# Attention scores over the 32 rows of a head pair, head-tile scores issued in turn with the next pair's tail-tile scores

## The chip, the cores and the metric

The kernel runs on one core of a Trainium2 chip. The metric is the time of one execution on the device, in microseconds (us), and the median of several runs is compared. The engines are called TensorE (PE in the profile, with its weight loads as PEld), VectorE (DVE), ScalarE (ACT), GpSimd (POOL) and SyncE (SP).

## What is computed

One block of a transformer in the "macaron" form: half a mixture-of-experts feed-forward, attention, and half the same feed-forward again. The input is 4 batches x 256 tokens x 256 features. The change touches the attention alone:

```
q = (x @ w_q.T).reshape(b, t, 16, 16)      # 16 heads of 16 features
k = (x @ w_k.T).reshape(b, t, 16, 16)
v = (x @ w_v.T).reshape(b, t, 16, 16)
scores = einsum('bqhd,bkhd->bhqk', q, k)
scores = where(causal, -inf, scores)
attn = softmax(scores / sqrt(256), axis=-1)
ctx = einsum('bhqk,bkhd->bqhd', attn, v).reshape(b, t, 256)
x = x + ctx @ w_o.T + b_o
```

## The kernel before

**Stages.** The first feed-forward fills the span up to about 175 us, the attention lies between 175 and 303 us, and the second feed-forward follows. Each engine has its own instruction list, written out by hand; a list is worked off in its order, and `wait_ge` on a semaphore holds an engine's list until another engine has counted far enough. `reach(eng, signal, count)` is the same wait, left out where the count is zero or less.

**Attention.** A batch has 256 queries and keys, which are two tiles of 128 queries. The first is called the head tile here: it sees 128 keys at most. The second, the tail tile, sees all 256. The 256 features of q and k lie on partitions in two chunks `c` of 128; a chunk holds 8 heads of 16 rows, so four pairs of heads (`CPAIRS` = 4), and a batch has 8 pairs (`HPAIRS`). Products in full precision are made from three matmuls: high part times high part, high times low, low times high.

**Steps.** `sweep` runs `step` for batch 0 on its own, in a loop for batches 1 to 3 (with the rest of the batch before in it), and once more for what is left. A step handles pieces of several pairs, shifted against each other. In step `s` TensorE does, in this order:

- `scores(b, s, True)`: the tail scores of pair `s - 2` (`SLAG` is 2), three matmuls of 512 columns at line 1483 (two heads x 256 keys) into bank 0 or 1, and the causal mask as a fourth matmul at line 1484;
- `turn_probs`: six transposes (line 1494) of the probabilities of pair `s - 4`;
- in steps 0 and 3, `chunk`: eight matmuls (line 1450) for a chunk of q and k of the next batch into bank 7;
- `scores(b, s, False)`: the head scores of pair `s - 2`, three matmuls of 256 columns and a mask into bank 2;
- `weigh`: 18 small matmuls (lines 1509 to 1511) of probabilities and values of pair `s - 5`.

In step 6 follow four transposes of the context (`turn_context`, line 1523) and at the start of step 7 eight matmuls of the output projection (`project_out`, line 1530).

**The other engines in a step.** VectorE: maximum of the tail scores (line 1143), maximum of the head scores (1147), and `low` (1156), the low parts of the turned probabilities; in step 5 first `add_up` (1164, 1166). ScalarE, in this order: `exps` of the tail (line 787, two instructions and their accumulator reads), in steps 0 and 3 the copies of k and q (773, 774), `exps` of the head (line 795, likewise two), then `high` (line 805), which copies the turned probabilities of the pair that TensorE turns in step `s + 1`. In step 6 the context's copy (line 815) comes ahead of the tail's exponentials. GpSimd: `mask_keys` (line 617) makes `k_head` for a pair, four instructions for high and low part and the two heads. The stationary operand is a whole chunk of q, 128 rows, so `k_head` holds the chunk's keys with all rows but the head's 16 set to zero (`head_mask`). Two slots of `k_head` are used in turn (`KSLOTS`).

**Buffers.** The tail scores have banks 0 and 1 in turn, the head scores bank 2 alone. The waits that follow from it in `scores` are

```
reach(pe, tail_probs_ready, g * 2 - 2)     # tail: the pair before the last has left its bank
reach(pe, head_probs_ready, g * 2)         # head: the last pair's exponentials have read bank 2
```

where `g` counts the pairs and each pair counts the semaphore up by two, once for each head.

Of the kernel before, what the change touches and what calls it, by code (L numbers as in the profile page):

```python
# [54 lines left out]
CONSTS = 20  # L55
IDENT_CONSTS = 3
KSLOTS = 2
# [7 lines left out]
SUM_STEP, OUT_STEP = 5, 6  # L65
POOL_LEAD = 1
# [9 lines left out]
def build(nc, x_in, wq_in, wk_in, wv_in, wo_in, bo_in, wr_in, win_in, wout_in, bias_in, out):  # L76
    with ExitStack() as ctx:
# [21 lines left out]
        with ExitStack() as room:  # L99
# [8 lines left out]
            with ExitStack() as inner_room:  # L108
                k_head = [inner_room.enter_context(nc.sbuf_tensor(f"k_head{u}", [P, 2, 2, SEQ], F32R)) for u in range(KSLOTS)]
# [90 lines left out]
        head_mask = sb("head_mask", [P, HPC])  # L200
        minus_half = sb("minus_half", [P, TILES])
# [258 lines left out]
        def _(pool):  # L460
# [44 lines left out]
            select(head_mask[:, :], [[HD, HPC]], HD - 1, -1, ALU.is_ge, 0.0)  # L505
            assert steps[0] == CONSTS

# [97 lines left out]
            def mask_keys(b, s):  # L605

                g = b * HPAIRS + (s - SLAG)
                p = (s - SLAG) % HPAIRS
                c = p // CPAIRS
                chunks = (b * DK + (c + 1 - (DK if s < SLAG else 0)))  # L610

                reach(pool, head_scored, g + (1 - KSLOTS))
                for part, (k, ready) in enumerate(((k_hi, k_hi_ready), (k_lo, k_lo_ready))):
                    pool.wait_ge(ready, chunks)
                    for hh in range(2):
                        h = 2 * p + hh
# [20 lines left out]
        def _(act):  # L637
# [139 lines left out]
            def exps(b, s, tail):  # L777

                g = b * HPAIRS + (s - SLAG)
                p, u = (s - SLAG) % HPAIRS, s % 2  # L780
                batch = b if s >= SLAG else b - 1
# [27 lines left out]
            def step(b, old, new):  # L809
                for s in range(HPAIRS):  # L810
# [14 lines left out]
                    if old if s < SLAG else new:  # L825
                        exps(b, s, False)
# [26 lines left out]
        def _(dve):  # L853
# [282 lines left out]
            def maxima(b, s, tail):  # L1136

                g = b * HPAIRS + (s - SLAG)
                u = s % 2
# [50 lines left out]
            def step(b, old, new):  # L1190
                for s in range(HPAIRS):
# [6 lines left out]
                    if old if s < SLAG else new:  # L1198
# [46 lines left out]
        def _(pe):  # L1245
# [217 lines left out]
            def scores(b, s, tail):  # L1463

                g = b * HPAIRS + (s - SLAG)
                c, u = (s - SLAG) % HPAIRS // CPAIRS, s % 2
                keys = k_head[s % KSLOTS]
# [153 lines left out]
```

## Time and profile before

| | us |
|---|---|
| median of three runs | 452.99 |
| the three runs | 454.75, 452.99, 451.97 |
| span of the profiled execution | 448.6 |
| TensorE busy | 401.3 (89%) |
| VectorE busy | 302.4 (67%) |
| GpSimd busy | 269.0 (60%) |
| ScalarE busy | 257.7 (57%) |

The span goes from the first to the last instruction; the profiled execution's own device time isn't given apart, so the span is set beside the median, which is 4.4 us above it. Matmuls overlap, and their ends are modelled: the distance between the starts of two matmuls says more than the busy time.

### The profile page before, as it was taken

Reading aid. Unit: us, or ns where it says so; the run is one execution under the profiler, and the core shown is the slowest. Engines: PE = TensorE matmul, PEld = TensorE weight load, DVE = VectorE, ACT = ScalarE, POOL = GpSimd, SP = SyncE. Lnnn points to the kernel's source line nnn. Section 1 sums busy time; section 2 is a strip of 40 time slices with the busy share of each in tenths; the row PEclk is TensorE's granted clock in tenths of the full one; section 3 lists DMA queues with packets and bytes.
Section 4 is the critical chain, followed back from the end, with each engine's and each line's share of the span. In section 5 each row is a group of like instructions: output and inputs, shape, how many; then the busy total and the mean of one; then the engine's idle time right before and its main releaser. Section 6 shows DMA issues by size and latency. Waiting matters only on the chain.

```text
span 448.6 us, 10288 instructions
## 1 busy us (share of the span) xinstructions
PE 401.3 (89%) x2892; PEld 330.1 (74%) x2893; DVE 302.4 (67%) x605; ACT 257.7 (57%) x630; POOL 269.0 (60%) x314
## 2 busy tenths in 40 slices
PE   7305999999999989889999999988899999999995
PEld 3302788888888876758788888766478888888884
DVE  6795855685565688697767677775556576655656
ACT  2561656555655645688778788832065565565552
POOL 5846874686547817857757777410255576755760
PEclk9555899999999999999999999998899999999999
DMA  8748841111212180000000000004571112211136
GB/s 276 287 187 300 282 136 58 47 57 37 70 49 49 43 273 8 1 1 3 4 0 0 0 0 0 1 1 153 162 249 53 54 35 70 59 58 47 47 85 222
DMA packets 25736, 38.87 MB, mean 87 GB/s; under 512 B 3056, under 2 KB 20720, under 8 KB 25712
## 3 DMA queue, kind: packets, MB, share of 16 engines
q1 hardware_dynamic: 19088, 24.41, 16.1%
q0 software_dynamic: 4544, 12.07, 8.9%
q10 hardware_dynamic: 2080, 2.10, 1.4%
q8 instruction: 12, 0.20, 0.2%
q14 instruction: 12, 0.10, 0.1%
HBM read 29.37 MB, written 9.19 MB: 86 GB/s over the span
## 4 chain that ended last, share of the span: by engine, by line
PE 65%; DVE 16%; DMA 7%; POOL 3%; ACT 3%; issue 3%; SPq 0%; DVEq 0%; ACTq 0%; POOLq 0%
PE bank L1326 24%; PE bank L1348 12%; PE bank L1483 7%; PE bank L1494 4%; PE bank L1336 4%; DMA arena<-xn_scratch,gather_row 3%; PE bank L1450 2%; PE bank L1302 2%; PE bank L1249 2%; DMA w_out<-y_scratch 2%; PE bank L1530 2%; DVE w_lo L892 2%; POOL w_lo L511 2%; DMA y_scratch<-arena,scatter_row 1%; PE bank L1484 1%
## 5 line engine op out<-in xcount | busy, mean ns | idle before, releaser
L524 POOL DMA_INDIRECT arena<-xn_scratch,gather_row x46 | 52.8, 1149 | 58.1 <-PE bank L1302 35.6
L530 POOL DMA_INDIRECT y_scratch<-arena,scatter_row x42 | 59.3, 1412 | 31.6 <-ACT arena L701 28.6
L1326 PE MATMUL bank<-w_hi,xT_hi 128*128 x184 | 62.4, 420 | 2.1 <-ACT xT_hi L664 2.1
L1018 DVE TENSOR_TENSOR wo_lo<-w_out,wo_hi 128x1024 fp32r<-128x1024 f32 x46 | 62.0, 1348 | 2.9 <-PE bank L1348 2.0
L1023 DVE TENSOR_TENSOR gT_lo<-bank,gT_hi 128x512 fp32r<-128x512 f32 x46 | 31.7, 690 | 45.4 <-ACT gT_hi L679 45.4
L1326 PE MATMUL bank<-w_lo,xT_hi 128*128 x184 | 58.0, 396 | 0.0
L1326 PE MATMUL bank<-w_hi,xT_lo 128*128 x184 | 57.8, 395 | 0.0
L617 POOL TENSOR_TENSOR k_head<-k_hi,head_mask 128x256 fp32r<-128x256 f32 x64 | 38.8, 627 | 28.8 <-PE bank L1484 21.7
L690 ACT ACTIVATE wo_hi<-w_out 128x1024 fp32r x46 | 48.8, 1061 | 9.5 <-issue 8.7
L672 ACT ACTIVATE arena<-bank 128x512 f32<-128x512 f32 x46 | 27.5, 598 | 42.9 <-PE bank L1326 42.9
L1007 DVE TENSOR_TENSOR xT_lo<-bank,xT_hi 128x256 fp32r<-128x256 f32 x46 | 19.5, 424 | 43.0 <-ACT xT_hi L664 43.0
L1483 PE MATMUL bank<-k_head,xT_hi 128*128 128x256 f32 (+1 forms) x128 | 39.8, 392 | 1.9 <-ACT probs L795 1.2
L1326 PEld LDWEIGHTS bank<-w_hi,xT_lo 128*128 128x128 f32 x184 | 34.8, 189 | 8.3 <-DVE xT_lo L1007 0.2
L1326 PEld LDWEIGHTS bank<-w_lo,xT_hi 128*128 128x128 f32 x184 | 34.8, 189 | 8.0
L617 POOL TENSOR_TENSOR k_head<-k_lo,head_mask 128x256 fp32r<-128x256 f32 x64 | 38.3, 620 | 0.6 <-DVE k_lo L1130 0.6
L701 ACT ACTIVATE arena<-bank 128x256 f32<-128x256 f32 x42 | 16.2, 385 | 39.1 <-PE bank L1348 39.1
L787 ACT ACTIVATE probs<-bank,neg_max 128x256 f32<-128x256 f32 x64 | 29.9, 479 | 8.7 <-DVE neg_max L1143 8.6
L1348 PE MATMUL bank<-wo_hi,gT_hi 128*128 128x256 f32 x184 | 33.0, 301 | 1.4 <-ACT gT_hi L679 1.4
L805 ACT ACTIVATE pT_hi<-bank 128x384 f16<-128x384 f32 x64 | 28.0, 488 | 10.4 <-PE bank L1494 10.3
L1156 DVE SCALAR_TENSOR_TENSOR pT_lo<-bank,pT_hi 128x384 f16<-128x384 f32 x64 | 32.4, 548 | 0.6
L1326 PEld LDWEIGHTS bank<-w_hi,xT_hi 128*128 128x128 f32 x184 | 29.0, 194 | 3.5 <-issue 3.1
L1032 DVE TENSOR_TENSOR arena<-arena,bank 128x512 f32<-128x512 f32 x46 | 31.1, 677 | 0.4 <-issue 0.4
(180 smaller groups left out, 979.9 us busy)
## 6 DMA issues: line engine op xcount, KB each, us to landing
w_out<-in_win_t SPq DMA_DIRECT2D x8, 1024.0 KB, 5.1
w_out<-in_wout_t SPq DMA_DIRECT2D x16, 512.0 KB, 6.0
w_out<-y_scratch SPq DMA_DIRECT2D x16, 256.0 KB, 4.4
xn_scratch<-arena ACTq DMA_DIRECT2D x2, 1024.0 KB, 6.1
x<-in_x SPq DMA_DIRECT2D x4, 256.0 KB, 3.7
out<-x SPq DMA_DIRECT2D x4, 256.0 KB, 2.2
arena<-xn_scratch,gather_row POOLq DMA_INDIRECT x46, 3.4
y_scratch<-arena,scatter_row POOLq DMA_INDIRECT x46, 3.0
```

What stands on the lines that cost most here:

```text
L524: pool.indirect_dma_start(out=xb[j % 2][:, :], out_offset=None, in_=xn_dram, in_offset=bass.IndirectOffsetOnAxis(ap=gather_row[:, j:j + 1] ...
L530: pool.indirect_dma_start(out=y_dram, in_=y[j % 2][:, :], in_offset=None, out_offset=bass.IndirectOffsetOnAxis(ap=scatter_row[:, j:j + 1], ...
L617: ins = pool.tensor_tensor(k_head[s % KSLOTS][:, part, hh, :], k[:, c, :].bitcast(F32), head_mask[:, h % HPC:h % HPC + 1].to_broadcast([P, ...
L690: act.activation(wo_hi[u][:, :, :], w_out[:, bass.ds(e, 1), :, :].rearrange("p o c d -> p (o c) d"), ACT.Copy)\
L787: act.activation(probs[u][:, hh, 1:3, :], bank[u][:, hh * SEQ:(hh + 1) * SEQ].rearrange("p (k t) -> p k t", k=2), ACT.Exp, bias=neg_max[u] ...
L1018: dve.tensor_tensor(wo_lo[:, :, :], w_out[:, bass.ds(e, 1), :, :].rearrange("p o c d -> p (o c) d"), wo_hi[u][:, :, :].bitcast(F32), ALU.s ...
L1023: dve.tensor_tensor(gT_lo[:, :, :], bank[4][:, :].rearrange("p (c t) -> p c t", c=HK), gT_hi[:, :, :].bitcast(F32), ALU.subtract).then_inc ...
L1032: dve.tensor_tensor(g[:, :], sa[:, :], bank[2 + u][:, :], ALU.mult).then_inc(g_done, 1)
L1156: dve.scalar_tensor_tensor(pT_lo[u][:, :, :], bank[3 + hh][:, 0:3 * P].rearrange("p (k t) -> p k t", k=3), P_SCALE, pT_hi[u][:, :, :], ALU ...
L1326: last = pe.matmul(bank[2 * half + u][:, :], tok[u][:, k, :], wts[:, bass.ds(e, 1), k, half * H:(half + 1) * H], start=(part == 0 and k == ...
L1348: last = pe.matmul(bank[y_bank(j)][:, 0:D], tok[:, c, :], wts[:, c, :], start=(part == 0 and c == 0), stop=(part == 2 and c == HK - 1))
L1483: pe.matmul(to, q[:, 1 if tail else 0, :], keys[:, part, :, 0:width], start=(n == 0), stop=False)
```

## The change

Four edits:

- `k_head` is now made for a chunk, not for a pair. `parity_mask` has two columns: ones in the rows of all even heads, and ones in those of all odd heads. `mask_keys(b, c)` runs in steps 0 and 3 only, four instructions for four pairs. Three small GpSimd instructions at the start build the mask (`CONSTS` goes from 20 to 23). `k_head` has one buffer for each chunk, as large in all as before.
- The scores are products over the 32 rows of the pair within the chunk: both operands are cut to `rows`. Other pairs' rows are left out by the cut, the other head of the pair by the mask.
- The head scores come one step later (`HEAD_LAG` = 1): step `s` has the tail scores of pair `s - 2` and the head scores of pair `s - 3`, whose maxima and exponentials move by one step with them.
- Both are issued by one call at the start of the step: first all waits of both, then tail, head, tail, head, tail, head, tail mask, head mask. The pairs of a step are neighbours, so they lie in different groups of 32 rows.

```diff
-            def mask_keys(b, s):
-                g = b * HPAIRS + (s - SLAG)
-                p = (s - SLAG) % HPAIRS
-                ...
-                reach(pool, head_scored, g + (1 - KSLOTS))
+            def mask_keys(b, c):
+                reach(pool, head_scored, b * HPAIRS + (CPAIRS * (c + 1) - HPAIRS))
                 for part, (k, ready) in enumerate(((k_hi, k_hi_ready), (k_lo, k_lo_ready))):
-                    pool.wait_ge(ready, chunks)
+                    pool.wait_ge(ready, b * DK + (c + 1))
                     for hh in range(2):
-                        ins = pool.tensor_tensor(k_head[s % KSLOTS][:, part, hh, :], k[:, c, :].bitcast(F32),
-                                                 head_mask[:, h % HPC:h % HPC + 1].to_broadcast([P, SEQ]), ALU.mult)
+                        ins = pool.tensor_tensor(k_head[c][:, part, hh, :], k[:, c, :].bitcast(F32),
+                                                 parity_mask[:, hh:hh + 1].to_broadcast([P, SEQ]), ALU.mult)
...
-                    if old if s < SLAG else new:
-                        mask_keys(b, s)
+                    if new and s in CHUNK_STEP:
+                        mask_keys(b, CHUNK_STEP.index(s))
...   # ScalarE's exps and VectorE's maxima
-                g = b * HPAIRS + (s - SLAG)
+                at = s - SLAG - (0 if tail else HEAD_LAG)
+                g = b * HPAIRS + at
...
-                    if old if s < SLAG else new:
+                    if old if s < SLAG + HEAD_LAG else new:
                         exps(b, s, False)
...
+            def scores(b, s, tail, head):
                 mask = bc(neg_mask[:, :], 1, [P, 2, P])
+                jobs = []
                 if tail:
+                    at = s - SLAG
+                    g, p = b * HPAIRS + at, at % HPAIRS
+                    chunks = b * DK + (p // CPAIRS + 1 - (DK if at < 0 else 0))
+                    if p % CPAIRS == 0:
+                        pe.wait_ge(qk_ready, chunks)
+                        pe.wait_ge(k_head_ready, chunks)
                     reach(pe, tail_probs_ready, g * 2 - 2)
+                    jobs.append((bank[s % 2][:, :].rearrange("p (h k) -> p h k", h=2), p, 1, SEQ, tail_scored))
+                if head:
+                    at = s - SLAG - HEAD_LAG
+                    g, p = b * HPAIRS + at, at % HPAIRS
                     reach(pe, head_probs_ready, g * 2)
+                    jobs.append((bank[2][:, 0:2 * P].rearrange("p (h k) -> p h k", h=2), p, 0, P, head_scored))
+                for n, (q, part) in enumerate(((q_hi, 0), (q_hi, 1), (q_lo, 0))):
+                    for to, p, tile, width, _ in jobs:
+                        c, rows = p // CPAIRS, slice(p % CPAIRS * ROWS, p % CPAIRS * ROWS + ROWS)
+                        pe.matmul(to, q[c][rows, tile, :], k_head[c][rows, part, :, 0:width], start=(n == 0), stop=False)
+                for to, _, _, width, scored in jobs:
+                    pe.matmul(to[:, :, width - P:width], ident_b[:, :], mask, start=False, stop=True).then_inc(scored, 1)
...   # TensorE's step
-                    if old if s < SLAG else new:
-                        scores(b, s, True)
+                    scores(b, s, old if s < SLAG else new, old if s < SLAG + HEAD_LAG else new)
...   # after chunk(...)
-                    if old if s < SLAG else new:
-                        scores(b, s, False)
```

## Rows read from the trace of the kernel before

**Rows 1.** Page, part 1: busy time of each engine.
```profile
PE 401.3 (89%) x2892; PEld 330.1 (74%) x2893; DVE 302.4 (67%) x605; ACT 257.7 (57%) x630; POOL 269.0 (60%) x314
```
**Rows 2.** Windows: length, busy time and (instructions) of each engine, PEclk, DMA share, GB/s.
```profile
202.00:216.00 14.00, 14.00 (x147) 11.78 (x145) 9.96 (x20) 12.22 (x49) 9.70 (x17) 1.00 0.01 2
...
300.00:380.00 80.00, 75.99 (x462) 60.85 (x463) 47.48 (x116) 36.89 (x65) 37.44 (x30) 0.96 0.34 109
```
**Rows 3.** Timeline of TensorE, steps 1 and 2 of batch 1: start us, us, what.
```profile
206.96 0.71 PE L1483 MATMUL bank<-k_head,xT_hi 128*128 128x512 f32 x2
...
207.74 0.28 PE L1484 MATMUL bank<-neg_mask,ident_b 128*128 128x256 bf16 x1
207.86 0.82 PE L1494 MATMUL bank<-ident,probs 128*128 128x128 f32 x6
208.44 0.48 PE L1483 MATMUL bank<-k_head,xT_hi 128*128 128x256 f32 x2
...
208.88 0.28 PE L1484 MATMUL bank<-neg_mask,ident_b 128*128 128x256 bf16 x1
...
209.45 0.71 PE L1483 MATMUL bank<-k_head,xT_hi 128*128 128x512 f32 x2
...
211.00 0.50 PE L1483 MATMUL bank<-k_head,xT_hi 128*128 128x256 f32 x2
```
**Rows 4.** Timeline of ScalarE, same steps.
```profile
208.47 0.87 ACT L805 ACTIVATE pT_hi<-bank 128x384 f16<-128x384 f32 x2 [0.41 <-PE bank L1494]
...
209.23 0.48 ACT L787 ACTIVATE probs<-bank,neg_max 128x256 f32<-128x256 f32 x1
...
210.13 0.38 ACT L795 ACTIVATE probs<-bank,neg_max 128x128 f32<-128x128 f32 x1
...
210.72 0.23 ACT L795 ACTIVATION_READ_ACCUMULATOR probs<-bank,neg_max  x1
```
**Rows 5.** Timeline of VectorE, same steps.
```profile
208.17 0.69 DVE L1143 TENSOR_REDUCE neg_max<-bank 128x2 f32<-128x512 f32 x1 [0.38 <-PE bank L1484]
```
**Rows 6.** Waits of TensorE, 176 to 292 us: total us, times, longest.
```profile
PE bank L1483 <- ACT probs L795: 1.2, 1, 1.2
```
**Rows 7.** Timeline of TensorE, step 5 of batch 1: first small matmul, next tail scores.
```profile
221.50 0.19 PE L1509 MATMUL bank<-v,pT_hi 128*128 x1
...
222.82 0.49 PE L1483 MATMUL bank<-k_head,xT_hi 128*128 128x512 f32 x1
```
**Rows 8.** Timeline of TensorE and ScalarE, step 3 of batch 1: the chunk.
```profile
213.92 1.03 PE L1450 MATMUL bank<-arena,wq 128*128 x4
...
215.85 0.39 ACT L773 ACTIVATE k_hi<-bank 128x256 fp32r<-128x256 f32 x1 [0.20 <-PE bank L1450]
...
216.13 0.38 ACT L774 ACTIVATE xT_hi<-bank 128x256 fp32r<-128x256 f32 x1
```
**Rows 9.** Timeline of ScalarE, step 6 of batch 1: the context's copy.
```profile
225.10 0.60 ACT L815 ACTIVATE wv<-bank 128x512 f32<-128x512 f32 x1
225.58 0.49 ACT L787 ACTIVATE probs<-bank,neg_max 128x256 f32<-128x256 f32 x1
```
**Rows 10.** Timeline of TensorE: first tail scores of step 0, batch 1 and last sweep.
```profile
202.69 0.71 PE L1483 MATMUL bank<-k_head,xT_hi 128*128 128x512 f32 x2
...
284.87 0.71 PE L1483 MATMUL bank<-k_head,xT_hi 128*128 128x512 f32 x2
```
**Rows 11.** Timeline of TensorE and ScalarE, batch 0: tail scores of step 6, step 5's last exponentials.
```profile
195.77 0.71 PE L1483 MATMUL bank<-k_head,xT_hi 128*128 128x512 f32 x2
...
198.86 0.21 ACT L795 ACTIVATION_READ_ACCUMULATOR probs<-bank,neg_max 128x1 f32 x1
```
**Rows 12.** Timeline of TensorE, last sweep: last pair's probabilities turned.
```profile
292.92 0.99 PE L1494 MATMUL bank<-ident,probs 128*128 128x128 f32 x6
```
**Rows 13.** Page, part 5: a group of the key masks, count, busy us, mean ns, idle before.
```profile
L617 POOL TENSOR_TENSOR k_head<-k_hi,head_mask 128x256 fp32r<-128x256 f32 x64 | 38.8, 627 | 28.8 <-PE bank L1484 21.7
```
**Rows 14.** Timeline of GpSimd at the start: constants done, first work after them.
```profile
12.40 0.45 POOL L472 TENSOR_SCALAR_AFFINE_SELECT head_mask<-head_mask 128x8 f32<-128x8 f32 x2
13.52 7.94 POOL L511 TENSOR_TENSOR w_lo<-w_out,w_hi 128x1024 fp32r<-128x1024 f32 x3 [0.66 <-ACT w_hi L657]
```

More of the change, by code:

```diff
@@ L54 @@
 STAGES = 3
-CONSTS = 20
+CONSTS = 23
 IDENT_CONSTS = 3
-KSLOTS = 2
+ROWS = 2 * HD
 P_SCALE = 2.0 ** 15
@@ L65 @@
 SUM_STEP, OUT_STEP = 5, 6
+HEAD_LAG = 1
 POOL_LEAD = 1
@@ L108, in build @@
             with ExitStack() as inner_room:
-                k_head = [inner_room.enter_context(nc.sbuf_tensor(f"k_head{u}", [P, 2, 2, SEQ], F32R)) for u in range(KSLOTS)]
+                k_head = [inner_room.enter_context(nc.sbuf_tensor(f"k_head{c}", [P, 2, 2, SEQ], F32R)) for c in range(DK)]
             xnT_late = room_sb("xnT_late", [P, DK, T])
@@ L505, in _ @@
             select(head_mask[:, :], [[HD, HPC]], HD - 1, -1, ALU.is_ge, 0.0)
+            then(pool.tensor_tensor(parity_mask[:, :], head_mask[:, 0:2], head_mask[:, 2:4], ALU.add))
+            for h in range(4, HPC, 2):
+                then(pool.tensor_tensor(parity_mask[:, :], parity_mask[:, :], head_mask[:, h:h + 2], ALU.add))
             assert steps[0] == CONSTS
@@ L777, in exps @@
             def exps(b, s, tail):
-                g = b * HPAIRS + (s - SLAG)
-                p, u = (s - SLAG) % HPAIRS, s % 2
-                batch = b if s >= SLAG else b - 1
+                at = s - SLAG - (0 if tail else HEAD_LAG)
+                g = b * HPAIRS + at
+                p, u = at % HPAIRS, at % 2
+                batch = b if at >= 0 else b - 1
                 if tail:
@@ L1136, in maxima @@
             def maxima(b, s, tail):
-                g = b * HPAIRS + (s - SLAG)
-                u = s % 2
+                at = s - SLAG - (0 if tail else HEAD_LAG)
+                g = b * HPAIRS + at
+                u = at % 2
                 if tail:
@@ L1197, in step @@
                         low(b, s)
-                    if old if s < SLAG else new:
+                    if old if s < SLAG + HEAD_LAG else new:
                         maxima(b, s, False)
@@ L1461, in values @@
                     last.then_inc(v_done, 1)
[L1463 to L1467, printed above, removed]
+            def scores(b, s, tail, head):
                 mask = bc(neg_mask[:, :], 1, [P, 2, P])
+                jobs = []
                 if tail:
-                    if (s - SLAG) % CPAIRS == 0:
-                        pe.wait_ge(qk_ready, b * DK + (c + 1 - (DK if s < SLAG else 0)))
-                    pe.wait_ge(k_head_ready, g + 1)
+                    at = s - SLAG
[4 more added lines that the diff above has]
+                        pe.wait_ge(k_head_ready, chunks)
@@ L1475, in scores @@
                     reach(pe, tail_probs_ready, g * 2 - 2)
-                    to = bank[u][:, :].rearrange("p (h k) -> p h k", h=2)
-                else:
+                    jobs.append((bank[s % 2][:, :].rearrange("p (h k) -> p h k", h=2), p, 1, SEQ, tail_scored))
+                if head:
+                    at = s - SLAG - HEAD_LAG
+                    g, p = b * HPAIRS + at, at % HPAIRS
                     reach(pe, head_probs_ready, g * 2)
-                    to = bank[2][:, 0:2 * P].rearrange("p (h k) -> p h k", h=2)
@@ L1481, in scores @@
-                width = SEQ if tail else P
-                for n, (q, part) in enumerate(((q_hi[c], 0), (q_hi[c], 1), (q_lo[c], 0))):
-                    pe.matmul(to, q[:, 1 if tail else 0, :], keys[:, part, :, 0:width], start=(n == 0), stop=False)
-                pe.matmul(to[:, :, width - P:width], ident_b[:, :], mask, start=False, stop=True)\
-                    .then_inc(tail_scored if tail else head_scored, 1)
+                    jobs.append((bank[2][:, 0:2 * P].rearrange("p (h k) -> p h k", h=2), p, 0, P, head_scored))
```

5 lines of the change are left out of this document (1 added, 4 removed).

## The prediction

> **What bounds the kernel now.** I read the page first: TensorE is busy for 89% of the span, far ahead of the others [rows 1]. That is a mean, so I cut the span into windows by stage. In the attention's loop TensorE shows 14.00 us of work in 14.00 us at the full clock, ScalarE 12.22 and VectorE 9.96 [rows 2]. Read alone, this says: take work from TensorE. The timeline of one step tells how far that holds. Tail scores start at 206.96 and the next step's at 209.45, which is 2.49 us; inside, tail matmuls take 0.78, their mask 0.12, the transposes 0.58, the head's three matmuls 0.44, all as distances between starts [rows 3]. So TensorE issues without a gap and paces this step.
>
> The same rows show a second thing, and the forecast rests on it. The tail scores that start at 206.96 are followed by VectorE's maximum, which begins at 208.17 [rows 5]; ScalarE first does the copies of the turned probabilities (208.47), then the exponentials of these tail scores (209.23), then those of the head scores (210.13), and the last accumulator read ends at 210.72 + 0.23 = 210.95 [rows 4]. The head scores of the *next* step start at 211.00 [rows 3]: they wait for bank 2 to be read. From tail scores of one step to head scores of the next the chain takes 4.04 us. It fits in a 2.49 us rhythm because the head scores stand 1.48 us into their step (208.44 - 206.96), behind transposes that have something else to do: 2.49 + 1.48 = 3.97 are on offer, and 4.04 are wanted. It is just met; in one place of batch 0 it isn't, and TensorE waits 1.2 us for those exponentials [rows 6].
>
> **The change part by part.**
>
> *The moved wait.* The new `scores` first waits for everything that tail and head need, and then issues both. One of these waits is `head_probs_ready` for the pair before: ScalarE's head exponentials of step s-1. ScalarE makes them behind the tail exponentials of step s-1, and these need the tail scores of step s-1. Hence the scores of step s can't start before the whole chain from the scores of step s-1 has run. Queued behind that wait on TensorE are the next tail scores, the transposes, the chunk and the small matmuls; ScalarE's copies wait for the transposes, and its next tail exponentials stand behind the copies. The lag of one step doesn't help: it moves maxima and exponentials along with the head scores. What was 4.04 us spread over one step and the 1.48 us of the next becomes a cycle that closes once a step.
>
> *Its length in a plain step*, counted from the start of the scores:
> - Scores to transposes. If the head matmuls run inside the tail's, it is 0.78 + 0.12 + 0.12 = 1.02 [rows 3]. If they run one after the other, 0.44 more: 1.46. No row shows matmuls over 32 rows, nor a change from such a form to the 128-row masks. A bound for one change is what a matmul still has in the array when the next starts: the mask lasts 0.28 and is followed after 0.12, so 0.16; into the 32-row form TensorE comes from a wait, out of it at full cost. Bounds: 0.90 (head mask hidden too) to 1.46 + 2 x 0.16 = 1.78. I take 1.02 + 0.16 = 1.18, as the two jobs have different rows and banks.
> - First transpose to ScalarE's copy: 208.47 - 207.86 = 0.61; copies until tail exponentials: 209.23 - 208.47 = 0.76 [rows 3, 4]. The tail's maximum isn't later: scores' mask at 0.78, VectorE 0.43 behind its start, 0.69 long, gives 1.90 [rows 3, 5] against 1.18 + 1.37 = 2.55.
> - Tail and head exponentials: 210.95 - 209.23 = 1.72 [rows 4]; back to TensorE 211.00 - 210.95 = 0.05 [rows 3, 4].
>
> Sum: 1.18 + 0.61 + 0.76 + 1.72 + 0.05 = 4.32 us, against 2.49. TensorE's own work in it is 1.18 + 0.58 and the small matmuls. Those took 1.32 us for 18 where TensorE had no instructions queued (221.50 to 222.82 [rows 7]), so they end at about 3.1 us and are hidden.
>
> The Trainium skill bears on the first item twice. "TensorE: Matmul & The Clock Gate", Part 3: Packing small matmuls, has matmuls in different 32-row strips start some 4 ns apart; "TensorEngine Tiling (Array Packing)", Key Properties, says that changing the tiling mode drains the engine, which speaks against a kernel that goes in and out of it once a step. By the first alone the item is 1.02, and the second has no price there. No row of this trace shows either.
>
> *Chunk steps (0 and 3).* ScalarE's copies of k and q stand between tail and head exponentials and wait for the chunk's matmuls: these start after the transposes, at 1.18 + 0.58 = 1.76; the first copy is 215.85 - 213.92 = 1.93 behind, two copies take twice 216.13 - 215.85 = 0.28 [rows 8]; then 0.82 for the head exponentials (210.95 - 210.13 [rows 4]) and 0.05. Sum 5.12.
>
> *Step 6.* The context's copy stands ahead of the tail exponentials and delays them by 225.58 - 225.10 = 0.48 [rows 9]: 4.80. The output projection falls into TensorE's free time.
>
> *One pass of the loop:* 5 x 4.32 + 2 x 5.12 + 4.80 = 36.64 us. Before: (284.87 - 202.69) / 3 = 27.39 [rows 10]. That is +9.25, and +27.7 for three passes. VectorE's `add_up` in step 5, which held the small matmuls of [rows 7] back, is now hidden; the absolute sum has this in it.
>
> *Batch 0.* Until step 5 VectorE's work on the values sets the pace in both kernels. The scores of step 6 then wait for step 5's head exponentials, which end at 198.86 + 0.21 = 199.07, some 0.6 earlier without head scores in step 2 (an estimate), where the tail scores started at 195.77 [rows 11]: +2.7. Steps 6 and 7 take 2 x 4.32 = 8.64 in place of 202.69 - 195.77 = 6.92: +1.7. Together +4.4.
>
> *Last sweep.* From step 0 to the turning of the last pair's probabilities it was 292.92 - 284.87 = 8.05 [rows 10, 12]. Now two steps (8.64), the head scores alone with mask and one change (0.44 + 0.12 + 0.16), transposes to copies to exponentials (0.61 + 0.76 + 0.82) and 0.05: 11.60, so +3.5. All of the rest up to the second feed-forward hangs on it.
>
> *Key masks.* GpSimd made 128 instructions of some 0.62 us [rows 13] and now makes 32. That frees about 60 us, none of it on the path: GpSimd idled ahead of them, waiting for head scores. A chunk's four take 2.5 us and are needed two steps later in step 2, three steps later in step 6. Zero, and a slight gain on VectorE at most.
>
> *Three constants at the start.* GpSimd idles 0.66 us between the last constant and the first weight split [rows 14]; the last two constants took 0.45 together, so three take some 0.68. Zero, and at most these 0.68 if the split doesn't wait for ScalarE as it does now.
>
> **Sum.** 27.7 + 4.4 + 3.5 = 35.6. The profiled span becomes 448.6 + 35.6 = 484.2, and by the median, 4.4 above the span, 452.99 + 35.6 = 488.6 us.
>
> **Rivals.**
>
> *A. TensorE stays the bound, and the head matmuls vanish inside the tail's.* This is the reading of [rows 1, 2], and where the skill's overlap would lead if nothing else closed: 0.44 x 32 steps = 14 us, 439 us. It decides if the exponentials of step s-1 are over before TensorE reaches the scores of step s, so if the chain were at most 2.05 us (2.49 - 0.44). The rows give 4.04 for the chain as it is. Against it: everything. For it: only that I could misread an order. Chance 0.04. Changed within 1% (chain loosely met, gains and losses cancel): 0.03.
>
> *B. The matmuls over 32 rows run one after the other, with drains both ways.* The step is 4.32 + (1.78 - 1.18) = 4.92. Over 24 steps of the loop, and about 5 around it, 0.60 x 29 = 17 us more: 506 us. For it: no row of this trace shows two matmuls side by side in the array. Chance 0.20. In this case most of the scores' rows in the trace would start one tail or head length apart.
>
> *C. The clock falls.* TensorE would be idle for a third of each step. In 300 to 380 us, where routing leaves it idle, the mean granted clock is 0.96 in place of 1.00 [rows 2]. At the lower level (1.2 GHz) scores and transposes of a step, 1.18 + 0.3 before ScalarE's first copy, would take twice as long: +1.5 x 29 = 43 us, 532 us. Against it: idle stretches of 1.2 us a step are short, and work comes back each time. Chance 0.05.
>
> *D. The chain as forecast*, with the scores' item anywhere between 0.90 and 1.4: chance 0.68. Its own range: 0.90 makes 0.28 x 29 = 8 us less, 480; a shorter chain where GpSimd is quiet takes 3 more, 477; the upper end 0.22 x 29 = 6 more, 495.
>
> **How the numbers follow.** Slower by over 1%: D, B and C, 0.93. A measurement of this kernel can tell about 1% from no change. The range leaves out A, the null and C, some 0.12, and reaches over B: 477 to 506.
>
> **What the profile of the changed kernel would show.** Tail scores 4.3 us apart in plain steps and 5.1 in steps 0 and 3; once a step TensorE idle ahead of its scores, released by ScalarE's head exponentials (`probs`); a chain that changes engine four times a step (TensorE scores and transposes, ScalarE) in place of TensorE alone; GpSimd's masks at 32. Tail and head matmuls starting close together show the overlap (else B). The feed-forwards must be unchanged. The prediction is wrong if steps run under 4 us, or if the head exponentials end before TensorE has finished its small matmuls.

## The result and the profile after

| | before | after |
|---|---|---|
| median, us | 452.85 (4 runs, 451.97 to 454.75) | 524.12 (4 runs, 522.11 to 525.93) |
| profiled span, us | 448.6 | 523.3 |
| mean granted clock of TensorE | 0.954 | 0.840 |

The ratio is 1.159, with a 95% interval of 1.155 to 1.163. The change costs 71 us; 35.6 were forecast, and the time lies above the range of 477 to 506. The direction and the new cycle came as forecast; the other half of the loss is TensorE's clock, which the sum had left at full speed.

**The page.** TensorE's busy time [rows 1], the clock in 40 slices, the shares of the chain, one group of key masks [rows 13] and the scores' group:

```profile
PE 434.4 (83%) x2892; PEld 352.9 (67%) x2893; DVE 304.2 (58%) x605; ACT 260.0 (50%) x630; POOL 213.5 (41%) x221
...
PEclk9556999999999995766766675775879999999999
...
PE 61%; DVE 13%; ACT 10%; DMA 7%; issue 5%; POOL 3%; ACTq 1%; SPq 0%; DVEq 0%; POOLq 0%
...
L1488 PE MATMUL bank<-k_head,xT_hi 32*128 32x256 f32 (+1 forms) x128 | 32.5, 509 | 47.1 <-ACT probs L795 46.9
...
L616 POOL TENSOR_TENSOR k_head<-k_hi,parity_mask 128x256 fp32r<-128x256 f32 x16 | 9.5, 615 | 123.2 <-ACT k_hi L772 123.2
```

TensorE has the same 2892 instructions as before and is busy for 33 us more: that points to the same work at a lower speed. The clock row shows where. In the slices from 196 us to the end of the last scores it reads 5 to 7 in place of 9. The last two rows show that the scores' matmuls wait 47 us in all for ScalarE's head exponentials, and that a group of masks is down from 64 instructions to 16.

**Windows by stage**, columns as in [rows 2]. First the loop of the kernel before, from step 0 of batch 1 on; then the changed kernel's batch 0, loop and last sweep:

```profile
202.70:284.80 82.10, 81.41 (x856) 67.70 (x852) 57.98 (x120) 66.02 (x256) 59.34 (x103) 1.00 0.00 1
```
```profile
180.30:211.10 30.80, 22.40 (x154) 17.05 (x154) 18.41 (x36) 18.59 (x69) 4.82 (x5) 0.74 0.01 1
211.20:352.10 140.90, 105.44 (x852) 83.38 (x852) 60.71 (x120) 67.53 (x255) 17.54 (x30) 0.68 0.00 0
352.20:367.40 15.20, 11.53 (x95) 8.96 (x95) 7.19 (x16) 6.92 (x26) 0.00 (x0) 0.50 0.01 1
```

Of the 74.7 us between the spans, 58.9 lie in the loop, 6.7 in batch 0 (24.1 to 30.8), 7.2 in the last sweep (8.0 to 15.2), 1.7 before the attention and 0.2 behind it. VectorE's and ScalarE's busy time in the loop is nearly that of before (60.7 for 58.0, 67.5 for 66.0); TensorE's rises from 81.4 to 105.4 at a mean clock of 0.68.

**The timeline of TensorE** shows two steps in a row, as [rows 3]; of the small matmuls only the last one of the first step is shown:

```profile
235.74 0.70 PE L1488 MATMUL bank<-k_head,xT_hi 32*128 32x512 f32 x4 [1.10 <-ACT probs L795]
236.08 0.59 PE L1488 MATMUL bank<-k_head,xT_lo 32*128 32x256 f32 x2
236.60 0.39 PE L1490 MATMUL bank<-neg_mask,ident_b 128*128 128x256 bf16 x2
236.83 0.82 PE L1499 MATMUL bank<-ident,probs 128*128 128x128 f32 x6
...
237.92 0.18 PE L1516 MATMUL bank<-v,pT_lo 128*128 x1
240.06 1.19 PE L1488 MATMUL bank<-k_head,xT_hi 32*128 32x512 f32 x4 [1.97 <-ACT probs L795]
...
241.61 0.61 PE L1490 MATMUL bank<-neg_mask,ident_b 128*128 128x256 bf16 x2
242.01 1.49 PE L1499 MATMUL bank<-ident,probs 128*128 128x128 f32 x6
...
245.78 0.76 PE L1488 MATMUL bank<-k_head,xT_hi 32*128 32x512 f32 x2 [1.80 <-ACT probs L795]
```

The first step takes 240.06 - 235.74 = 4.32 us, to the hundredth what was forecast. Scores to transposes are 1.09 in it (1.18 forecast): 0.86 for six products, 0.23 for two masks. Its last small matmul ends at 237.92 + 0.18 = 238.10, and TensorE then waits for 1.97 us. The second step takes 5.72 with the same instructions. Its products last 1.55, its masks 0.40, its transposes 1.49 in place of 0.82. The first step up to 239.60 and the second as windows:

```profile
235.74:239.60 3.86, 2.35 (x32) 1.86 (x32) 2.58 (x6) 2.16 (x9) 1.28 (x3) 1.00 0.01 2
240.06:245.78 5.72, 3.92 (x32) 3.06 (x33) 2.52 (x6) 2.59 (x10) 1.20 (x2) 0.50 0.01 3
```

The granted clock is 1.00 in the first and 0.50 in the second, the lower of the two levels (1.2 GHz). Each step has one block of tail and head scores; 19 of the 32 ran wholly at the lower level.

**The chain of waits** through the slow step, in order of time (start, us, what):

```profile
240.06 1.62 PE bank L1488 x4
241.68 0.54 PE bank L1490 x2
242.22 1.29 PE bank L1499 x6
...
244.28 0.66 ACT probs L787 x3
244.94 0.71 ACT probs L795 x4
245.65 0.14 issue
245.78 0.58 PE bank L1488
```

It is the cycle of the prediction: scores, transposes, ScalarE's copies, tail exponentials, head exponentials, scores. Between transposes and exponentials ScalarE's queue works through the copies, in short pieces that are left out here. In this cycle 3.45 us lie on TensorE (1.62 + 0.54 + 1.29), so the work that the lower clock stretches lies on the path.

### The profile page after: what moved, and what is told of

Its sections match the earlier page's. It is cut to its first block, busy times and chain, and to the rows that moved or that the text cites. A ratio compares the mean times of both kernels' runs of the same rounds, so it can differ in the third digit from the quotient of the medians.

```text
span 523.3 us, 10163 instructions
## 1 busy us (share of the span) xinstructions
PE 434.4 (83%) x2892; PEld 352.9 (67%) x2893; DVE 304.2 (58%) x605; ACT 260.0 (50%) x630; POOL 213.5 (41%) x221
## 4 chain that ended last, share of the span: by engine, by line
PE 61%; DVE 13%; ACT 10%; DMA 7%; issue 5%; POOL 3%; ACTq 1%; SPq 0%; DVEq 0%; POOLq 0%
PE bank L1327 21%; PE bank L1349 11%; PE bank L1488 8%; PE bank L1499 6%; ACT probs L795 4%; ACT probs L787 4%; PE bank L1451 3%; PE bank L1337 3%; DMA arena<-xn_scratch,gather_row 3%; PE bank L1490 3%; PE bank L1303 2%; DMA w_out<-y_scratch 2%; PE bank L1535 2%; DVE arena L879 1%; POOL w_lo L516 1%
## 5 line engine op out<-in xcount | busy, mean ns | idle before, releaser
L1488 PE MATMUL bank<-k_head,xT_hi 32*128 32x256 f32 (+1 forms) x128 | 32.5, 509 | 47.1 <-ACT probs L795 46.9
L805 ACT ACTIVATE pT_hi<-bank 128x384 f16<-128x384 f32 x64 | 30.7, 490 | 81.5 <-PE bank L1499 79.3
L1144 DVE TENSOR_REDUCE neg_max<-bank 128x2 f32<-128x512 f32 x32 | 22.1, 691 | 72.1 <-PE bank L1490 72.1
L616 POOL TENSOR_TENSOR k_head<-k_hi,parity_mask 128x256 fp32r<-128x256 f32 x16 | 9.5, 615 | 123.2 <-ACT k_hi L772 123.2
L1488 PEld LDWEIGHTS bank<-k_head,xT_hi 32*128 32x128 f32 x128 | 14.5, 257 | 51.6 <-ACT probs L787 32.5
L1499 PE MATMUL bank<-ident,probs 128*128 128x128 f32 x192 | 42.0, 382 | 0.0
L1157 DVE SCALAR_TENSOR_TENSOR pT_lo<-bank,pT_hi 128x384 f16<-128x384 f32 x64 | 34.9, 556 | 10.7 <-ACT pT_hi L805 10.1
L1499 PEld LDWEIGHTS bank<-ident,probs 128*128 128x128 f32 x192 | 35.9, 205 | 1.4
```

The costliest lines, as they stand in the source:

```text
L805: act.activation(pT_hi[(s - 1) % 2 * 2 + hh][:, :, :], bank[3 + hh][:, 0:3 * P].rearrange("p (k t) -> p k t", k=3), ACT.Copy, scale=P_SCAL ...
L1157: dve.scalar_tensor_tensor(pT_lo[u][:, :, :], bank[3 + hh][:, 0:3 * P].rearrange("p (k t) -> p k t", k=3), P_SCALE, pT_hi[u][:, :, :], ALU ...
L1488: pe.matmul(to, q[c][rows, tile, :], k_head[c][rows, part, :, 0:width], start=(n == 0), stop=False)
L1499: last = pe.transpose(bank[3 + hh][:, i * P:(i + 1) * P], probs[s % 2][:, hh, i, :], ident[:, :])
```

## The experiments

Each kernel was run beside the kernel before on the same chip, and each ratio is against it; the rounds were on different chips, where the kernel before took 452.9 to 453.9 us. "128 rows" means that the products run over all rows of the chunk, so that scores of four pairs are summed; such a kernel is a probe and nothing to use.

### Is the cycle the chain through ScalarE, and what opens it?

**e4: head exponentials a step earlier.** ScalarE does them ahead of its copies, VectorE takes the head's maximum first; TensorE's list is that of the changed kernel.

```diff
@@ ScalarE's step @@
-                    if old if s < SLAG + HEAD_LAG else new:
-                        exps(b, s, False)
...
+                    if old if s + 1 < SLAG + HEAD_LAG else new:
+                        exps(b, s + 1, False)
                     if old if s < SLAG + 1 else new:
                         high(b, s)
@@ VectorE's step @@
+                    if old if s < SLAG + HEAD_LAG else new:
+                        maxima(b, s, False)
                     if old if s < SLAG else new:
                         maxima(b, s, True)
...
-                    if old if s < SLAG + HEAD_LAG else new:
-                        maxima(b, s, False)
```

> The changed kernel with another order on two engines: VectorE takes the head's maximum before the tail's, and ScalarE makes the head exponentials of a step ahead of the copies of turned probabilities and of the tail exponentials. The joint wait stays. Theory: the cycle now holds scores (head mask issued at 0.97), 0.43 to the head's maximum, 0.42 for it, 0.13 to ScalarE, 0.82 for the head exponentials and 0.05 back: 2.8 us in place of 4.32. Plain steps of 2.8 to 3.0 us, clock over 0.93, 446 to 460 us. Rival (it is not this order on ScalarE that stretches the step): steps stay over 4 us, 515 us or more.

Measured: 469.22 us, ratio 1.035 (1.030 to 1.040). ScalarE's timeline has the new order, and the scores of one step and the next are 2.79 apart:

```profile
211.77 0.36 ACT L795 ACTIVATE probs<-bank,neg_max 128x128 f32<-128x128 f32 x1
...
212.12 0.87 ACT L805 ACTIVATE pT_hi<-bank 128x384 f16<-128x384 f32 x2
212.86 0.49 ACT L787 ACTIVATE probs<-bank,neg_max 128x256 f32<-128x256 f32 x1
```
```profile
212.42 0.69 PE L1488 MATMUL bank<-k_head,xT_hi 32*128 32x512 f32 x4 [0.50 <-ACT probs L795]
...
215.21 0.69 PE L1488 MATMUL bank<-k_head,xT_hi 32*128 32x512 f32 x4
```

So moving the head's two exponentials on ScalarE, and its maximum on VectorE, takes 1.5 us out of a step: the cycle is what the theory says. The total missed the expected 446 to 460, as the loop's mean clock is 0.85 and steps 0, 3, 5 and 6 take longer than summed.

**e1: the old place, 32 rows.** The head scores go back behind the chunk and lose their lag.

```diff
-HEAD_LAG = 1
+HEAD_LAG = 0
...
-                    scores(b, s, old if s < SLAG else new, old if s < SLAG + HEAD_LAG else new)
+                    scores(b, s, old if s < SLAG else new, False)
...
                         chunk(b, CHUNK_STEP.index(s))
+                    scores(b, s, False, old if s < SLAG + HEAD_LAG else new)
```

> Theory (the joint wait closes a cycle over TensorE, VectorE and ScalarE once a step, and the idle time that it makes lets the clock fall): with the head scores back in their old place behind transposes and chunk, for the same pair as the tail scores and with a wait of their own, while products over 32 rows and masks by parity stay, the cycle is open again. Plain steps of 2.5 to 2.8 us, clock as in the kernel before (0.95 or more over the span), 450 to 462 us: two changes of form a step may cost up to 0.16 us each. Rival (products over 32 rows are themselves what slows TensorE or lowers its clock): clock under 0.90 and over 475 us.

Measured: 468.03 us, ratio 1.032 (1.026 to 1.038), between what the two expected. **e5** is the same with the lag of one step kept.

> The changed kernel with the head scores back in their old place and with a wait of their own, but still one step late. Theory: the lag alone closes a cycle too, a shorter one: the transposes of step s need the head exponentials of step s-1, so 0.61 from the transposes' start to ScalarE's copies, 0.76, 1.72 for the exponentials and 0.05 make plain steps of 3.14 to 3.25 us at the full clock, between the 2.97 of the run without the lag and the 4.32 of the changed kernel; 474 to 490 us with some of the steps at the lower clock. Rival (only the joint wait matters, the lag is free): steps as in the run without the lag (2.97) and 464 to 471 us.

Measured: 472.69 us, ratio 1.044 (1.039 to 1.048), between the two ranges. Its plain steps are 2.96 us, those of e1 2.95 to 2.97, and the expected 3.14 to 3.25 is wrong. It took the transposes of a step to wait for both of the last step's head exponentials. In the kernel the first three wait for the first head's and the last three for the second's. Tail scores of one step, its two head exponentials' last reads, and the transposes of the next:

```profile
257.33 0.49 PE L1488 MATMUL bank<-k_head,xT_hi 32*128 32x512 f32 x1
...
260.86 0.23 ACT L795 ACTIVATION_READ_ACCUMULATOR probs<-bank,neg_max  x1
...
261.20 0.23 ACT L795 ACTIVATION_READ_ACCUMULATOR probs<-bank,neg_max  x1
...
261.31 0.82 PE L1499 MATMUL bank<-ident,probs 128*128 128x128 f32 x6
```

The first head's end at 261.09, 0.22 ahead of the transposes at 261.31; the second head's end at 261.43, and the fourth transpose starts at 261.63. So the lag closes a chain that is some 0.2 us shorter than the step, and TensorE sets the step as in e1. It is the joint wait at the start of the step that closes the long cycle. The lag isn't free all the same: e5's loop takes 99.0 us at a mean clock of 0.91, e1's 95.6 at 0.94, and no run shows why the clock is lower with it.

e1's timeline shows where its 0.48 us over the old 2.49 lie, by the distances of [rows 3]:

```profile
256.74 0.72 PE L1488 MATMUL bank<-k_head,xT_hi 32*128 32x512 f32 x2
...
257.63 0.28 PE L1490 MATMUL bank<-neg_mask,ident_b 128*128 128x256 bf16 x1
257.75 0.82 PE L1499 MATMUL bank<-ident,probs 128*128 128x128 f32 x6
258.50 0.50 PE L1488 MATMUL bank<-k_head,xT_hi 32*128 32x256 f32 x2
...
259.04 0.28 PE L1490 MATMUL bank<-neg_mask,ident_b 128*128 128x256 bf16 x1
```

Tail products to mask 0.89 (was 0.78), transposes to head scores 0.75 (0.58), head products to mask 0.54 (0.44), and from the small matmuls into the tail scores 0.53 (0.45). At each change between 32 and 128 rows 0.08 to 0.17 us are lost; between products of the same form the distances are those of before, within 0.02 us.

**e7: e1 with all 128 rows** (`rows` is `slice(0, P)`), to see whether that is the cause.

> Head scores in their old place and no lag, masks by parity once a chunk, and products over all 128 rows (so the scores of a chunk's even or odd heads are added up and the output is not the reference's). The run with 32 rows in this order had plain steps of 2.97 where the kernel before has 2.49. Theory: the 0.48 us are four changes of form a step, 0.08 to 0.17 each; with 128 rows they are gone, plain steps of 2.49 to 2.55 us, 449 to 456 us, clock 0.95 or more. Rival (the 0.48 us come from the masks by parity or from GpSimd's new timing): steps stay at 2.8 to 3.0, 462 us or more.

Measured: 450.00 us over 10 runs, ratio 0.994 (0.991 to 0.997). Plain steps are 2.49 again, at a clock of 1.00 in the whole loop. The 18 us between e1 and e7 belong to the 32 rows alone, through the changes of form (0.48 us a step) and through the clock (0.94 in e1's loop). e7 is the changed kernel's key masks, three more constants and nothing else of the change: these cost nothing measurable, and the two together are 0.6% faster than the kernel before.

### Where do the other 37 us come from?

**e3: matmuls into the pause.** Seven matmuls that nobody reads go into bank 7 behind the small ones, in four of the eight steps.

```diff
                         weigh(b, s)
+                    if new and s in (1, 2, 4, 5):
+                        pe.wait_ge(qk_ready, b * DK + (1 if s < CHUNK_STEP[1] else 2))
+                        warm(7, 7)
```

> The changed kernel with seven matmuls of 512 columns on constants behind the small matmuls of steps 1, 2, 4 and 5 of batches 0 to 3, into bank 7, which is free there (about 1.5 us at the full clock, inside the idle time of some 2 us). Theory: TensorE's idle time is what lets the clock fall, so the granted clock returns to 0.93 or more over the span and the kernel comes to 486 to 500 us, near what was forecast for the cycle at the full clock. Rival (the clock falls for the form of the score matmuls, or the time is lost elsewhere): clock stays under 0.88, 520 us or more.

Measured: 505.99 us, ratio 1.115 (1.109 to 1.121), above the expected 486 to 500. The filled stretch holds (from step 2 to step 7 plain steps take 4.26 to 4.36), and the clock still falls at steps 0 and 1, ahead of which steps 6, 7 and 0 had nothing filled in.

**e8: the same in every step**, into the tail bank that is free, more or fewer by the step's pause.

```diff
+                    if (new and (old or s >= 2)) or (old and s == 0):
+                        reach(pe, tail_probs_ready, (b * HPAIRS + (s + 1 - SLAG)) * 2 - 2)
+                        warm((5, 7, 7, 5, 7, 7, 2, 7)[s], (s + 1) % 2)
```

> The changed kernel with matmuls on constants in the idle time of every step of the attention (7 of 512 columns in plain steps, 5 in steps 0 and 3, 2 in step 6, into the bank of the next tail scores, which is free there). Theory: with idle time filled in steps 6, 7 and 0 too, the clock holds in all of them, every plain step takes 4.3 us, step 0 and 3 take 5.2, and the kernel comes to 484 to 494 us, the forecast for the cycle alone being 488.6. Rival (something else in step 0, which took 7.4 to 8.4 us, makes it long): step 0 stays over 7 us and the kernel over 500 us.

Measured: 488.61 us, ratio 1.079 (1.073 to 1.085); span 486.6. The loop's window and the fill in a step:

```profile
210.10:321.20 111.10, 104.35 (x993) 69.84 (x993) 58.27 (x120) 65.09 (x255) 17.55 (x30) 1.00 0.00 1
```
```profile
229.22 0.69 PE L1488 MATMUL bank<-k_head,xT_hi 32*128 32x512 f32 x4
...
231.42 1.67 PE L1250 MATMUL bank<-ones 128*128 128x512 f16 x7
```

141 more matmuls in the loop and 36.7 us less (523.3 - 486.6), 29.8 of them in the loop's windows. Plain steps take 4.31 to 4.33, step 7 4.25 to 4.35. Batch 0 and the last sweep give back 6.1 us more, so 35.9 us come from the attention; the rest is differences ahead of it and behind it. So the clock cost the changed kernel some 36 us, and what is left over the kernel before is the cycle.

**e10: the same fill over 32 rows**, the rows of the next tail pair.

```diff
+            def warm_rows(at, n, into):
+                for _ in range(n):
+                    pe.matmul(bank[into][:, :], ones[at:at + ROWS, :], bc(ones[at:at + ROWS, :], 1, [ROWS, 512 // P, P]), start=True, stop=True)
```

> The filled run (488.6 us, clock held through the attention), with the same fill, as many matmuls of 512 columns in the same places, but each over 32 rows in place of 128. TensorE is busy for as long. Theory (time without matmuls lets the clock fall): clock holds, 487 to 493 us. Rival (how many rows the matmuls use counts too, which would explain why the run with all 128 rows in the joint order kept the clock up for longer than the changed kernel although both have the idle time, and why the run in the old place lost it in places without idle time): steps at the lower clock come back, 5.7 us each, and the kernel takes 500 us or more.

Measured: 509.13 us, mean clock 0.909. The four runs spread from 502.55 to 511.74, so no ratio is given; the lowest is still 13.7 us above e11 below, which was run beside it with the same fill over 128 rows. Seven fill matmuls take 1.68 us here and 1.67 in e8. TensorE is busy for 97% of the loop, and the granted clock is 0.84:

```profile
211.00:340.00 129.00, 125.16 (x1000) 83.89 (x998) 59.47 (x121) 67.10 (x262) 17.55 (x30) 0.84 0.00 1
```

As many matmuls of as many columns as in e8, but over a quarter of the array's rows, hold the clock up only in part. So the time without matmuls isn't all that counts: it is 3% of the loop here and 6% in e8. Intermediate numbers of rows weren't tried.

**e2: the changed kernel with 128 rows**, its pauses left as they are.

```diff
-                        c, rows = p // CPAIRS, slice(p % CPAIRS * ROWS, p % CPAIRS * ROWS + ROWS)
+                        c, rows = p // CPAIRS, slice(0, P)
```

> The changed kernel, but each score product over all 128 rows of the chunk, so that the scores of all even or all odd heads of the chunk are added up and the output is not the reference's; instructions, order and waits are the same. Theory: the cycle stays; tail and head matmuls can't run side by side, so scores to transposes takes 1.46 in place of 1.09 us and a plain step at the full clock 4.7 in place of 4.32 us; the clock falls in it much as before, 525 to 545 us. Rival (products over 32 rows count less for the clock): clock over 0.93 and 490 to 505 us, faster than the changed kernel though its matmuls take longer.

Measured: 509.62 us, ratio 1.128 (1.123 to 1.134). The theory wanted 525 to 545, and it fell; the rival's 490 to 505 and its clock of 0.93 (0.919 measured) were just missed as well. Plain steps are longer at the full clock (4.58), as products of tail and head now take 1.12 to 1.14 in place of 0.86; even so the kernel is 14.5 us faster, because the loop's clock is 0.91 in place of 0.68. **e6** is e4 with 128 rows.

> The run with head maximum and exponentials first (469 us), with products over all 128 rows (output not the reference's, as the scores of a chunk's even or odd heads are added up). Theory (idle time): scores to transposes takes 1.36 in place of 1.09, plain steps 3.0 to 3.1 in place of 2.8, and the clock falls about as often: 472 to 480 us. Rival (rows count for the clock): it falls in few steps or none, and the kernel comes to 456 to 466 us although each step at the full clock is longer.

Measured: 467.55 us, ratio 1.027 (1.021 to 1.033), under the theory's range and 1.6 us above the rival's. The loop's windows of e6 and of e4 (32 rows), in this order:

```profile
203.40:297.30 93.90, 81.36 (x852) 69.68 (x853) 57.99 (x119) 64.39 (x256) 17.59 (x30) 1.00 0.00 1
```
```profile
203.40:301.20 97.80, 87.92 (x854) 69.53 (x852) 58.15 (x119) 64.56 (x255) 17.55 (x30) 0.85 0.00 1
```

e6 has 12.5 us of pauses in the loop and a longer plain step (3.07 for 2.8), and its clock doesn't fall in the loop. With 32 rows it does, with 9.9 us of pauses. The reverse is seen in e1:

```profile
206.10:301.70 95.60, 95.14 (x856) 71.46 (x852) 58.33 (x120) 66.31 (x254) 17.55 (x30) 0.94 0.00 1
```

TensorE is busy without a pause and the clock is 0.94, where e7, the same with 128 rows, has 1.00. Pauses and few rows both lower it: few rows without pauses gave 0.94 (e1), the changed kernel's pauses with 128 rows 0.91 (e2), and both together 0.68.

### Do matmuls over 32 rows overlap only in turn?

**e11: e8 with the tail's three products ahead of the head's three.**

```diff
-                for n, (q, part) in enumerate(((q_hi, 0), (q_hi, 1), (q_lo, 0))):
-                    for to, p, tile, width, _ in jobs:
+                for to, p, tile, width, _ in jobs:
+                    for n, (q, part) in enumerate(((q_hi, 0), (q_hi, 1), (q_lo, 0))):
```

> The filled run, but the three tail products are issued ahead of the three head products, not in turn with them; rows, banks and waits are the same. Measures what issuing in turn is worth at a held clock. If products over different rows overlap only when they are neighbours, 0.86 us from first product to mask become 0.86 + some 0.3, steps go from 4.32 to 4.6, and 498 us result; if they don't overlap in the changed kernel at all, nothing changes: 4.32 and 488 us.

Measured: 488.83 us, ratio 1.076 (1.070 to 1.083), as e8. The time is the one expected if nothing overlaps, but the products do overlap, which neither case had foreseen: from the first to the mask it is 218.34 to 219.20 = 0.86, as in turn. Narrow windows of its timeline give the last products of one step, one by one:

```profile
218.65 0.39 PE L1488 MATMUL bank<-k_head,xT_hi 32*128 32x512 f32 x1
218.69 0.27 PE L1488 MATMUL bank<-k_head,xT_lo 32*128 32x256 f32 x1
...
218.88 0.39 PE L1488 MATMUL bank<-k_head,xT_lo 32*128 32x512 f32 x1
219.20 0.28 PE L1490 MATMUL bank<-neg_mask,ident_b 128*128 128x256 bf16 x1
```

The head's third product (256 columns, `xT_lo`) starts at 218.69, the tail's third (512 columns) at 218.88, though the tail's stands ahead in the list. In e8, issued in turn, the starts come in the same order as here; in e2, over 128 rows, they come in the order of the list. Different rows are enough; issuing in turn is worth nothing.

### Is there a version that beats the kernel before?

**e9** puts a fill of one to five matmuls a step into e4, behind the transposes. Its edit lost the last sweep's warming matmuls and their wait.

> The run with the head's maximum and exponentials first, with a few matmuls on constants in the idle time (2 of 512 columns in most steps, 5 in step 5, 1 in steps 0 and 3). Theory: that run lost its time to steps at the lower clock (469 us); with the clock held, plain steps of 2.8, step 5 of 4.1, steps 0 and 3 of 4.1 and step 6 of 5.0 us give a pass of 28 us against 27.4 before, so 448 to 458 us, a tie with the kernel before. Rival (the fill delays the scores more than the clock gives back): 465 us or more.

Measured: 462.35 us, ratio 1.021 (1.016 to 1.025), between the two expected ranges. The loop's clock is 1.00 and plain steps are 2.80 to 2.84, but a pass is 30.3 us, longer than expected in steps 0, 1, 3 (4.3, 3.2, 4.3) and 6 (5.9). **e12** has those matmuls again.

```diff
                         if not new and s >= SLAG:
 
                             pe.wait_ge(attn_added, BATCH)
                             warm(WARM_END, 7)
+                    if (new and (old or s >= 2)) or (old and s == 0):
+                        reach(pe, tail_probs_ready, (b * HPAIRS + (s + 1 - SLAG)) * 2 - 2)
+                        warm((1, 2, 2, 1, 2, 5, 2, 2)[s], (s + 1) % 2)
```

> The kernel with the head's exponentials a step earlier and the fill (e9) had lost, by a slip in its edit, the warming matmuls that stand in the last sweep's steps 2 and 3 and their wait for the attention's sums. This one has them again. In e9 the 18.5 us behind the last sweep show a granted clock of 0.68, in the kernel without fill (e4) the same 18.5 us show 0.91. Theory: these matmuls are what keeps the clock there, the attention is as in e9 (passes of 30.3 us, loop at 1.00, plain steps 2.80 to 2.84), and with them the end gives back some 1 to 3 us: the kernel comes to 459 to 462 us, and still does not beat the kernel before, because its pass is 2.9 us longer, three times. Rival: they hold nothing at the end, and it stays at 462.4 within half a percent, or the wait that returns with them costs as much as they give.

Measured: 461.26 us, ratio 1.017 (1.014 to 1.020). The window behind the last sweep, e9 and then e12:

```profile
301.50:320.00 18.50, 15.25 (x107) 11.70 (x108) 11.78 (x51) 4.63 (x12) 2.03 (x2) 0.68 0.06 20
```
```profile
301.50:320.00 18.50, 15.62 (x135) 11.77 (x135) 12.56 (x54) 5.21 (x14) 2.04 (x2) 0.91 0.04 14
```

Its clock is back at 0.91, as expected. The medians differ by 1.1 us, about what a measurement can tell, and 461.26 fits the rival too (462.4 within half a percent); the profiled spans differ by 2.7. It is the fastest version found with products over 32 rows, and the kernel before is still faster by 1.4 to 2.0%.

## Why the prediction missed, and where it held

**What failed is the clock: the sum put its cost at nothing, and rival C got a chance of 0.05.** The reason given was "idle stretches of 1.2 us a step are short, and work comes back each time". The clock fell to its lower level in 19 of 32 blocks, and holding it up with matmuls that do nothing gave 36.7 us back (e8). The rival's price was near: 43 us were worked out, as +1.5 us in each of 29 steps. A slow plain step was 5.72 - 4.32 = 1.40 longer; fewer steps were slow, but the chunk's steps, partly at each level, lost more (7.1 to 8.4 against 5.2). Its 532 us stand beside 524 measured.

Three things went unseen. First, the idle stretch was too short in the forecast. It took 1.32 us for the small matmuls from a step in which VectorE held them back [rows 7] and let them end at about 3.1 us; they ended 2.36 us into the step, and TensorE waited 1.97 us and not 1.2. By [rows 3] they take only 0.45: from 208.88 + 0.12, behind the head's mask, to the next tail scores at 209.45. The cycle doesn't feel this, as they are off its path, but the argument against rival C rested on it. Second, the mean of 0.96 in a stretch with 5% of idle time [rows 2] was read as harmless. Third, the change takes rows from the matmuls, which by e10, by e2 against the changed kernel and by e6 against e4 lowers the clock as well. No row of before could show this third part; the first two spoke for a larger chance.

**The cycle: right, in place and size.** Joint wait, order of the links and the plain step of 4.32 came true in the steps at full clock and throughout e8, and e4 opened it by the order on ScalarE alone. The forecast's terms against e8, where the clock is held:

| term | forecast | e8 |
|---|---|---|
| scores to transposes | 1.18 | 1.09 |
| plain step | 4.32 | 4.31 to 4.33 (step 7: 4.25 to 4.35) |
| steps 0 and 3 | 5.12 | 5.28, 5.17 |
| step 6 | 4.80 | 5.03 |
| one pass | 36.64 | 37.03 |
| loop | +27.7 | +29.0 |
| batch 0 | +4.4 | +4.2 |
| last sweep | 11.60 | 11.59 |

That e8's median is the predicted 488.6 to a tenth is partly luck: its span is 486.6 and not 484.2, and its median lies 2.0 above the span, not 4.4. Before the attention e8 is 3.2 longer and behind it 1.9 shorter than the kernel before, for which no part of the change is a reason.

**Rival B: wrong.** Six products of tail and head take 0.86 with 32 rows and 1.12 to 1.14 with 128 (e2), so they do run side by side. This is what the Trainium skill's "TensorE: Matmul & The Clock Gate", Part 3: Packing small matmuls, lets one expect, and the traces agree: the first tail and head product start 0.01 us apart or less (e8, e11), and the gain is 0.26 us in a step that is then bound elsewhere. The bounds taken for a change of form, 0.16, were right: 0.08 to 0.17. The Trainium skill's "TensorEngine Tiling (Array Packing)", Key Properties, has the mode change drain the engine; e1 and e7 agree in that each change costs time, and give the price, 0.48 us a step with four changes. In the changed kernel there are two changes a step, and its 1.09 has them in it.

**Rival A and the lag.** Nothing supports A: with the cycle opened (e4, e12) the step is 2.8, still above 2.49. "The lag of one step doesn't help" held, and e5 adds that it doesn't lengthen a plain step either while the head scores stand late in the step.

**Key masks and constants: zero, as forecast** (e7, 450.0 against 453.0).

**What stays open.** How the 36.7 us divide between pauses and rows isn't settled: they don't simply add up (0.94 and 0.91 alone, 0.68 together), and e2's 14.5 us is the rows' part less the longer steps. Which pause in a pass brings the clock down wasn't singled out either, beyond e3's falls behind the unfilled steps 6 to 0. Nor was it tried to shorten steps 6, 0 and 3 of e12, where its remaining 2.9 us a pass lie.

## What to carry to other kernels

When two jobs are put behind one joint wait, follow each awaited signal to its place in the other engine's order: the later one's whole chain becomes a cycle, and here moving two instructions on that engine, and one on VectorE, was worth 1.5 us a step. Where a change gives TensorE pauses or fewer rows, price both levels of the clock before anything else: here scores and masks on the path took 1.95 us to the first transpose at the lower level and 1.09 at the higher; matmuls that nobody reads, put into the pause, tell in one run how much of a loss is the clock. With two products side by side 32 rows won 0.26 us a step and four changes of form cost 0.48; before going to 32 rows, weigh the two against each other.

## What the runs showed of the hardware

- The granted clock depends on how many rows the matmuls use: with the same number of fill matmuls, its mean over the loop was 1.00 over 128 rows (e8) and 0.84 over 32 rows (e10, TensorE busy for 97% of the loop).
- Pauses of 1.1 to 2.0 us in steps of 4.3 to 5.7 us were enough for a mean clock of 0.68 with 32-row scores; the same pauses with 128-row scores (e2) gave 0.91. With 128-row scores and 12.5 us of pauses in a loop of 93.9 us (e6) it stayed at 1.00.
- A change between 32 and 128 rows costs 0.08 to 0.17 us each way.
- Matmuls on different rows overlap whatever their order in the list: six products in 0.86 us in turn and in series (e8, e11), and in e11 the head's third starts 0.19 us ahead of the tail's third, which stands before it. Over 128 rows they start in the order of the list (e2).
